# Rows' first turns, a split of two groups' sums, and the last tiles' sums made in PSUM, in a float32 pipeline of attention, MLP and role adapters

## The chip, the cores and the metric

The kernel runs on one NeuronCore of a Trainium2 chip. Its five engines are TensorE (PE, matmuls; PEld is its weight loads), VectorE (DVE), ScalarE (ACT), GpSimd (POOL) and SyncE (SP, which issues most DMAs). They run their own instruction streams and meet only at semaphores. The metric is the device time of one launch in microseconds; lower is better.

## The reference

64 sequences of 32 rows and 256 features, all float32. First an attention block with an MLP after it, then three role adapters, one after another:

```python
attn_out = softmax((x@Wq)(x@Wk)^T * V**-0.5) @ (x@Wv) @ Wp + bp
cms_out  = gelu(attn_out @ cW1 + cb1) @ cW2 + cb2 + one_hot(target_codes)
modifier = gelu(concat[attn_out, cms_out] @ mW1 + mb1) @ mW2 + mb2
x = clip(x + cms_out + modifier, 0, 1)
for layer in range(3):                      # weights chosen by each sequence's role (3 roles)
    u = gelu(x @ W_down[role] + b_down[role]) @ W_up[role] + b_up[role]
    x = layernorm(x + u) * gamma[role] + beta[role]
```

V is 256, the MLP's hidden width is 1024, the adapters' is 128.

## The kernel before

**Order of the rows.** A short routing stage counts the sequences of each role and finds a place for every sequence, so that nearly all blocks of 128 rows (a "window", 16 of them) hold one role. POOL then gathers the rows of `x` in that order (`gather`, eight indirect DMAs of 128 rows for the first two groups, semaphore `half_in[n]` for each pair).

**Start on PE.** `turn_weights(0..2)` transposes Wq, Wk, Wv. `fold_weights(0)` makes Wq Wk^T, `fold_weights(1)` makes Wv Wp. `half_part("X", n)` transposes 256 gathered rows into a bank, ACT copies them to `xT`, and `half_part("Y", n)` multiplies them with the folded matrix. `keep_busy` is a matmul of the identity whose result nobody reads.

**Main part.** The MLP works feature-major (features on partitions, rows along the free axis) on five groups of rows, `GROUPS`: three of 512 rows and two of 256. Every product of two float32 matrices is made of three matmuls of high and low parts (`mm3`). For a group, PE walks a list written out by hand, `core`: `("H", n)` makes the hidden block n (0 to 7 of cW1, 8 to 15 of mW1), ACT makes its GELU and its high part, DVE its low part, and `("D", n)` multiplies it with cW2 or mW2. Hidden blocks 8 and up need both `attn_out` (first half of the sum, "Ha") and `cms_out` (second half, "Hb"). `("C", 0)` is ACT's and DVE's step in which `cms_out` leaves PSUM: two sums on DVE (`cms`), two copies on ACT (`cms_hi`), two differences on DVE (`cms_lo`). `("F", 0)` sums x + cms_out + modifier on DVE into `cms` (semaphore `mod_summed`), step E clips it into `xT` (semaphore `x1_ready`).

**Adapters.** While group g+1 is in the MLP, the four windows of group g go through the adapters in its gaps, at spots of the same list (`SPOT`, `HALF`): PE's `downs` and `ups`, ACT's GELU, DVE's norm and POOL's power -0.5. A window's first `down` waits for `x1_ready` (`x1_needed`). Windows 8 to 11 belong to the third group of 512 rows.

**The end.** The windows 13, 14 and 15 are the list `LAST`; each has an object `Last` (called `one`, `two_`, `three` in the code) with two PSUM banks, `sum_bank` and `turn_bank`. Their residual is summed by PE: `last_residual` multiplies the identity with `x` into `sum_bank` and `last_up` adds the adapter's output. For layer 0 that `x` comes from `last_first_sum` (PE transposes the clipped rows into `sum_bank`) and `last_sum` (DVE adds the up-bias, writes `tail.x`). Window 13 starts within the last group's MLP, the other two after it. Its weights, norm rows and up-bias take the places of slots 1 to 3 of the windows before, so SP loads them late (`first_of_last`, seven DMAs in a row, semaphore `loaded`, the up-bias last).

Of the kernel before, what the change touches and what calls it, by code (L numbers as in the profile page):

```python
# [8 lines left out]
ALU = mybir.AluOpType  # L9
# [3 lines left out]
P = 128  # L13
# [43 lines left out]
def build(nc, x, codes, roles, Wq, Wk, Wv, Wp, bp, cW1, cb1, cW2, cb2, mW1, mb1, mW2, mb2, adapters, out):  # L57
# [3 lines left out]
    with ExitStack() as ctx:  # L61
# [281 lines left out]
        core += [("D", HB - 2), ("Ha", HB), ("D", HB - 1), ("C", 0), ("Ha", HB + 1), ("Hb", HB), ("Hb", HB + 1)]  # L343
# [6 lines left out]
        for g in range(NM):  # L350
            for step in core:
# [4 lines left out]
                steps.append((g, step))  # L356
        ATTENTION = {0: {("H", 10): ("X", 2), ("H", 11): ("Y", 2), ("H", 13): ("S", 2), ("H", 14): ("P", 2),
# [86 lines left out]
        def x1_needed(w):  # L444
            return PRIMED + VB * next(n + 1 for n, (first, rows) in enumerate(GROUPS) if (w + 1) * P <= first + rows)
# [16 lines left out]
        def store_batches(engine, of_last, quarters):  # L462
# [4 lines left out]
            def go():  # L467
                engine.wait_ge(tail.x_ready, tail.base + LAYERS + 1)
# [232 lines left out]
        def _(act):  # L701
# [103 lines left out]
            def last_part(stage_name, tail, layer):  # L805
                if stage_name == "turn":
                    act.wait_ge(tail.turned, layer + 1)
                    act.activation(tail.xT[:, :, :], two(tail.turn_bank[:, 0:V]), ACT.Copy).then_inc(tail.xT_ready, 1)
# [8 lines left out]
            chunks(0, 1)  # L817
            folded_weights(1)
            act.wait_ge(bias_turned, 1)
            act.activation(bias[:, :], bank[3][:, 0:22], ACT.Copy).then_inc(bias_ready, 1)  # L820
            half_part("X", 0)
            chunks(1, 2)
            half_part("Y", 0)
            half_part("X", 1)
# [47 lines left out]
        def _(dve):  # L872
# [107 lines left out]
            def part(step, n, g):  # L980
# [24 lines left out]
                if step == "F":  # L1005
                    dve.wait_ge(h_used, PRIMED + 2 * HB * (g + 1))
                    dve.wait_ge(base_ready, VB * (g + 1))
                    for vb in range(VB):
                        dve.scalar_tensor_tensor(cms[:, vb, rows], result_banks(g, HB)[vb][:, rows], bias[:, MB2 + vb:MB2 + vb + 1],
                                                 xT[:, vb, cols], ALU.add, ALU.add).then_inc(mod_summed, 1)  # L1010
                if step == "E":
                    for vb in range(VB):
# [45 lines left out]
            def last_sum(tail):  # L1058
                dve.wait_ge(tail.loaded, 16 * tail.loads)
                dve.wait_ge(tail.turned, 1)  # L1060
                if tail.left:
                    dve.wait_ge(*tail.left)
                dve.tensor_tensor(tail.x[:, :], tail.sum_bank[:, 0:V], tail.up_bias[:, :], ALU.add).then_inc(tail.x_ready, 1)

            def last_stats(tail, layer):
# [10 lines left out]
            def last_norm(tail, layer):  # L1076
                dve.wait_ge(tail.norm_step, 3 * (tail.base + layer) + 3)
                dve.wait_ge(tail.rstd_ready, tail.base + layer + 1)
# [496 lines left out]
```

## Time and profile before

| what | us |
|---|---|
| runs timed (3) | 365.42, 366.13, 367.71, median 366.13 |
| profiled execution, whole | 363.89 |
| span of its instructions | 362.1 |
| PE busy | 348.7 (96%) |
| DVE / ACT / POOL busy | 197.0 / 166.4 / 62.0 |

The span goes from the first instruction to the last; the profiled execution took 1.8 us more than it. All rows are of this one execution, 2.2 us shorter than the median. In the rows of the timeline the columns are: start in us from the start of the span, length in us, engine, line, operation, output<-inputs, shape, how many, and in brackets the engine's idle time just before and what ended it. The end of a matmul is modelled: a matmul of 256 columns is listed as 0.28 us though the next one starts 0.12 us later, so lengths of neighbours overlap by about 0.16 us and a real pause of PE is that much longer than the bracket says.

### The profile page before, as it was taken

To read this page: it belongs to the slowest core of one execution; us is meant where nothing else is said; L and a number is where in the kernel's file an instruction comes from. 1 tells how busy PE (TensorE), PEld (TensorE's weight loads), DVE (VectorE), ACT (ScalarE), POOL (GpSimd) and SP (SyncE) were. 2 spreads that over 40 slices of the span, in tenths; PEclk is the share of its full clock that TensorE was granted. 3 is DMA by queue.
4 is the path that set the end of the run, shared out by engine and by line. 5 is a ranking of instruction groups with operands and counts; after the bars stand their busy time and mean duration, and the time that the engine had idled before them with its cause. 6 is when DMAs were issued, how large, how long until landed. Compare 5 with 4: busy or idle time off the path is not lost.

```text
span 362.1 us, 6606 instructions
## 1 busy us (share of the span) xinstructions
PE 348.7 (96%) x2232; PEld 282.9 (78%) x2232; DVE 197.0 (54%) x477; ACT 166.4 (46%) x333; POOL 62.0 (17%) x94
## 2 busy tenths in 40 slices
PE   7889999999999999999999999999999999999994
PEld 6677688677876867888786777877899999989962
DVE  5057365420332746763535766554579777553584
ACT  3465685432652555452326454443455554533421
POOL 2700230000040101001311111003322025100231
PEclk9999999999999999999999999999999999999999
DMA  6663799175020223220076797602856543298001
GB/s 209 202 229 119 200 106 162 11 213 130 2 58 0 60 80 97 69 79 0 29 242 159 208 264 241 172 29 80 207 151 191 160 107 98 66 295 310 16 2 44
DMA packets 30646, 46.14 MB, mean 127 GB/s; under 512 B 4779, under 2 KB 15348, under 8 KB 30612
## 3 DMA queue, kind: packets, MB, share of 16 engines
q1 hardware_dynamic: 28852, 41.72, 42.6%
q0 software_dynamic: 1392, 3.80, 3.6%
q8 instruction: 18, 0.29, 0.4%
q10 hardware_dynamic: 368, 0.20, 0.2%
q14 instruction: 16, 0.13, 0.1%
HBM read 43.60 MB, written 4.48 MB: 133 GB/s over the span
## 4 chain that ended last, share of the span: by engine, by line
PE 85%; ACT 5%; DVE 4%; issue 3%; POOL 2%; DMA 1%; POOLq 0%; DVEq 0%; ACTq 0%
PE bank L312 11%; PE bank L314 10%; PE bank L313 10%; PE bank L1353 8%; PE bank L1358 8%; PE bank L1354 7%; PE bank L1277 4%; PE bank L1397 4%; PE bank L1376 3%; PE bank L1228 2%; PE bank L1267 2%; PE bank L1248 2%; ACT h_full L760 2%; PE bank L1428 2%; ACT h_hi L764 1%
## 5 line engine op out<-in xcount | busy, mean ns | idle before, releaser
L760 ACT ACTIVATE h_full<-bank,bias 128x512 f32<-128x512 f32 (+1 forms) x80 | 48.2, 602 | 114.4 <-PE bank L314 109.6
L985 DVE TENSOR_TENSOR h_lo<-h_full,h_hi 128x512 fp32r<-128x512 f32 (+1 forms) x80 | 46.7, 584 | 65.1 <-ACT h_hi L764 63.6
L683 POOL TENSOR_TENSOR rstd<-moments,minus_half 128x1 f32<-128x1 f32 x39 | 24.3, 624 | 174.2 <-DVE moments L1039 174.2
L764 ACT ACTIVATE h_hi<-h_full 128x512 fp32r<-128x512 f32 (+1 forms) x80 | 43.7, 546 | 2.6
L1031 DVE TENSOR_TENSOR window_y<-bank,window_x 128x256 f32<-128x256 f32 x39 | 16.5, 423 | 42.6 <-PE bank L1376 34.8
L1353 PE MATMUL bank<-h_hi,m_hi 128*128 128x512 f32 (+1 forms) x80 | 31.1, 397 | 0.4 <-ACT h_hi L764 0.3
L1353 PE MATMUL bank<-h_hi,c_hi 128*128 128x512 f32 (+1 forms) x80 | 30.8, 395 | 0.1
L312 PE MATMUL bank<-at_hi,m_hi 128*128 128x512 f32 (+1 forms) x80 | 29.5, 369 | 0.0
L312 PE MATMUL bank<-at_hi,c_hi 128*128 128x512 f32 (+1 forms) x80 | 29.4, 367 | 0.0
L314 PE MATMUL bank<-at_lo,c_hi 128*128 128x512 f32 (+1 forms) x80 | 27.8, 348 | 0.0
L314 PE MATMUL bank<-at_lo,m_hi 128*128 128x512 f32 (+1 forms) x80 | 27.8, 347 | 0.0
L313 PE MATMUL bank<-at_hi,c_lo 128*128 128x512 f32 (+1 forms) x80 | 27.7, 347 | 0.0
L313 PE MATMUL bank<-at_hi,m_lo 128*128 128x512 f32 (+1 forms) x80 | 27.7, 346 | 0.0
L1354 PE MATMUL bank<-h_hi,c_lo 128*128 128x512 f32 (+1 forms) x80 | 27.2, 348 | 0.0
L1354 PE MATMUL bank<-h_hi,m_lo 128*128 128x512 f32 (+1 forms) x80 | 27.1, 348 | 0.0
L655 POOL DMA_INDIRECT xr<-in_x,row_idx x16 | 16.4, 1022 | 62.7 <-PE bank L1267 52.9
L312 PE MATMUL bank<-cms_hi,m_hi 128*128 128x512 f32 (+1 forms) x70 | 24.5, 350 | 0.0
L314 PE MATMUL bank<-cms_lo,m_hi 128*128 128x512 f32 (+1 forms) x70 | 24.5, 350 | 0.0
L313 PE MATMUL bank<-cms_hi,m_lo 128*128 128x512 f32 (+1 forms) x70 | 24.3, 347 | 0.0
L1358 PE MATMUL bank<-h_lo,c_hi 128*128 128x512 f32 (+1 forms) x80 | 21.7, 352 | 0.2
L1022 DVE SCALAR_TENSOR_TENSOR window_x<-window_y,rstd,adapter_rows 128x256 f32<-128x256 f32 x39 | 18.8, 481 | 5.4 <-POOL rstd L683 3.7
L1358 PE MATMUL bank<-h_lo,m_hi 128*128 128x512 f32 (+1 forms) x80 | 21.4, 349 | 0.0
(216 smaller groups left out, 717.9 us busy)
## 6 DMA issues: line engine op xcount, KB each, us to landing
adapter_w<-packed_w SPq DMA_DIRECT2D x48, 256.5 KB, 3.5
adapter_rows<-packed_rows SPq DMA_DIRECT2D x36, 256.0 KB, 3.7
mixed_w<-packed_w SPq DMA_DIRECT2D x12, 256.5 KB, 4.6
stage<-in_L_cond_mW SPq DMA_DIRECT2D x6, 512.0 KB, 4.7
stage<-in_L_cond_cW SPq DMA_DIRECT2D x4, 512.0 KB, 6.5
last_w<-packed_w SPq DMA_DIRECT2D x2, 769.5 KB, 5.8
up_bias<-in_L_cond_b_up SPq DMA_DIRECT2D x12, 128.0 KB, 5.5
adapter_rows<-packed_rows SPq DMA_DIRECT2D x24, 64.0 KB, 3.2
```

Source lines behind the costliest of these rows:

```text
L312: pe.matmul(o, w_hi_ap, r_hi_ap, start=first, stop=False)
L313: pe.matmul(o, w_lo_ap, r_hi_ap, start=False, stop=False)
L314: return pe.matmul(o, w_hi_ap, r_lo_ap, start=False, stop=last)
L683: pool.tensor_tensor(slot.rstd[:, :], slot.moments[:, 1:2], minus_half[:, :], ALU.pow)\
L760: act.activation(h_full[:, n % 2, rows], bank[n % 2][:, rows], ACT.Gelu, bias=bias[:, b:b + 1])\
L764: act.activation(h_hi[:, n % 2, rows], h_full[:, n % 2, rows], ACT.Copy).then_inc(h_hi_ready, 1)
L985: dve.tensor_tensor(h_lo[:, n % 2, rows], h_full[:, n % 2, rows], h_hi[:, n % 2, rows].bitcast(F32), ALU.subtract).then_inc(h_lo_ready, 1)
L1022: dve.scalar_tensor_tensor(slot.x[:, :], slot.y[:, :], slot.rstd[:, :], slot.rows[:, 1, :], ALU.mult, ALU.add).then_inc(slot.x_ready, 1)
L1031: dve.tensor_tensor(slot.y[:, :], bank[6][:, 0:V], slot.x[:, :], ALU.add).then_inc(emptied[6], 1)
L1353: pe.matmul(results[ob][:, rows], high(cols), h_hi[:, n % 2, rows], start=(j == 0), stop=False)
L1354: pe.matmul(results[ob][:, rows], low(cols), h_hi[:, n % 2, rows], start=False, stop=False)
L1358: ins = pe.matmul(results[ob][:, rows], high(cols), h_lo[:, n % 2, rows], start=False, stop=(j == HB - 1))
```

## The change

1. Start, PE: `half_part("X", 0)` goes ahead of `fold_weights(1)`, `half_part("X", 1)` ahead of `half_part("Y", 0)`; one `keep_busy` of 64 columns goes. ACT's list is moved in the same way.
2. Main list: block 8's first half ("Ha") moves from between D6 and D7 to behind D7 and C, in all five groups.
3. Sums and clips (F, E) of the third group and of the last one are made in two parts of half the rows each, clip right behind sum, and `x1_needed` counts parts.
4. The last windows: a matmul of the identity with the up-bias opens `sum_bank` (`last_bias`), a true matmul with the identity adds the turned rows (`last_first_sum`), DVE's `last_sum` and layer 0's `last_residual` go. Window 13's block moves from behind D8 of the last group to behind Hb9.

```diff
-        core += [("D", HB - 2), ("Ha", HB), ("D", HB - 1), ("C", 0), ("Ha", HB + 1), ("Hb", HB), ("Hb", HB + 1)]
+        core += [("D", HB - 2), ("D", HB - 1), ("C", 0), ("Ha", HB), ("Ha", HB + 1), ("Hb", HB), ("Hb", HB + 1)]
...
+        def sum_parts(g):
+
+            return 2 if g == NM - 1 or g + 1 in CARRIED and GROUPS[g][1] == GR else 1
...
-                if step == "E":
-                    for vb in range(VB):
-                        dve.wait_ge(mod_summed, VB * g + vb + 1)
-                        dve.tensor_scalar(xT[:, vb, cols], cms[:, vb, rows], 0.0, 1.0, ALU.max, ALU.min)\
-                            .then_inc(x1_ready, 1)
+                if step in ("F", "E"):
+                    share = size // sum_parts(g)
+                    for part_n in range(sum_parts(g)):
+                        rows = slice(part_n * share, (part_n + 1) * share)
+                        cols = slice(first + part_n * share, first + (part_n + 1) * share)
+                        if step == "F":
+                            for vb in range(VB):
+                                dve.scalar_tensor_tensor(cms[:, vb, rows], result_banks(g, HB)[vb][:, rows],
                                                         bias[:, MB2 + vb:MB2 + vb + 1], xT[:, vb, cols], ALU.add, ALU.add)\
                                    .then_inc(mod_summed, 1)
+                        if step == "E" or sum_parts(g) > 1:
+                            for vb in range(VB):
+                                dve.wait_ge(mod_summed, summed(g) + VB * part_n + vb + 1)
+                                dve.tensor_scalar(xT[:, vb, cols], cms[:, vb, rows], 0.0, 1.0, ALU.max, ALU.min)\
+                                    .then_inc(x1_ready, 1)
...
-            def last_sum(tail):
-                dve.wait_ge(tail.loaded, 16 * tail.loads)
...
-            keep_busy(1, P // 2)
...
+            def last_bias(n):
+                tail = last[n]
+                pe.wait_ge(tail.loaded, 16 * tail.loads)
+                pe.matmul(tail.sum_bank[:, 0:V], ident[:, :], tail.up_bias[:, :], start=True, stop=False)
+
             def last_first_sum(n):
                 tail, w = last[n], LAST[n]
                 for vb in range(VB):
-                    ins = pe.transpose(tail.sum_bank[:, vb * P:(vb + 1) * P], xT[:, vb, columns(w)], ident[:, :])
-                ins.then_inc(tail.turned, 1)
+                    pe.matmul(tail.sum_bank[:, vb * P:(vb + 1) * P], xT[:, vb, columns(w)], ident[:, :],
+                              start=False, stop=False)
...
-                if g == NM - 1 and step == ("D", HB):
+                if g == NM - 1 and step == ("Hb", HB + 1):
                     pe.wait_ge(cms_copied, VB * NM)
-                    pe.wait_ge(last[0].loaded, 16 * last[0].loads)
+                    last_bias(0)
                     pe.wait_ge(x1_ready, x1_needed(LAST[0]))
+                    last_first_sum(0)
                     last_down(0, 0)
-                    last_first_sum(0)
                 if g == NM - 1 and step == ("D", HB + 2):
-                    last_residual(0, 0)
                     last_up(0, 0)
```

PE at the start, from the last product of the routing stage on (`raw,wT` is fold_weights(1), `ident,xr` the rows' turns X, `xT,fold` the products Y). Before:

```order
L1206 MATMUL bank6<-onehot,own_id 1x12
L1169 MATMUL bank2<-raw,wT 128x256 x4
L1471 MATMUL bank3<-ident,bias_rows 128x22
L1219 MATMUL bank4<-ident,xr0 128x128 x4
L1228 MATMUL bank0<-xT,fold 128x256 x4
L1219 MATMUL bank5<-ident,xr0 128x128 x4
L1228 MATMUL bank1<-xT,fold 128x256 x4
```

and now:

```order
L1215 MATMUL bank6<-onehot,own_id 1x12
L1228 MATMUL bank4<-ident,xr0 128x128 x4
L1178 MATMUL bank2<-raw,wT 128x256 x4
L1486 MATMUL bank3<-ident,bias_rows 128x22
L1228 MATMUL bank5<-ident,xr0 128x128 x4
L1237 MATMUL bank0<-xT,fold 128x256 x4
L1237 MATMUL bank1<-xT,fold 128x256 x4
```

The first turn of rows stands ahead of the fold and of the biases' turn, and the two products Y follow each other.

PE in the last group, from the last matmul of hidden block 9 to the first of block 10 (the six of bank2 and bank3 are D8; bank4 and bank5 are window 13's banks). Before:

```order
L314 MATMUL bank1<-cms_lo,m_hi 128x256
L1353 MATMUL bank2<-h_hi,m_hi 128x256
L1354 MATMUL bank2<-h_hi,m_lo 128x256
L1353 MATMUL bank3<-h_hi,m_hi 128x256
L1354 MATMUL bank3<-h_hi,m_lo 128x256
L1358 MATMUL bank2<-h_lo,m_hi 128x256
L1358 MATMUL bank3<-h_lo,m_hi 128x256
L1455 MATMUL bank5<-xT,adapter_w2 128x128 x2
L1434 MATMUL bank4<-ident,xT 128x128 x2
L312 MATMUL bank0<-at_hi,m_hi 128x256
```

and now:

```order
L314 MATMUL bank1<-cms_lo,m_hi 128x256
L1443 MATMUL bank4<-up_bias1,ident 128x256
L1448 MATMUL bank4<-ident,xT 128x128 x2
L1469 MATMUL bank5<-xT,adapter_w2 128x128 x2
L1362 MATMUL bank2<-h_hi,m_hi 128x256
L1363 MATMUL bank2<-h_hi,m_lo 128x256
L1362 MATMUL bank3<-h_hi,m_hi 128x256
L1363 MATMUL bank3<-h_hi,m_lo 128x256
L1367 MATMUL bank2<-h_lo,m_hi 128x256
L1367 MATMUL bank3<-h_lo,m_hi 128x256
L312 MATMUL bank0<-at_hi,m_hi 128x256
```

Window 13's block stands ahead of D8, with a bias product (up_bias1) that waits for `loaded`; its layer 0 residual product (window_x1 with ident, two steps later) is gone.

PE behind the last MLP step (bank4 and bank5 are window 13's, bank0 and bank6 window 14's, bank1 and bank7 window 15's). Before:

```order
L1455 MATMUL bank5<-window_y2,adapter_w2 128x128 x2
L1463 MATMUL bank4<-adapter_w2,window_y3 128x256
L1455 MATMUL bank6<-xT,last_w1 128x128 x2
L1434 MATMUL bank0<-ident,xT 128x128 x2
L1455 MATMUL bank7<-xT,last_w2 128x128 x2
L1434 MATMUL bank1<-ident,xT 128x128 x2
L1448 MATMUL bank0<-last_x1,ident 128x256
L1463 MATMUL bank0<-last_w1,last_h1 128x256
L1448 MATMUL bank1<-last_x2,ident 128x256
L1463 MATMUL bank1<-last_w2,last_h2 128x256
```

and now:

```order
L1469 MATMUL bank5<-window_y2,adapter_w2 128x128 x2
L1443 MATMUL bank0<-last_up_bias1,ident 128x256
L1477 MATMUL bank4<-adapter_w2,window_y3 128x256
L1443 MATMUL bank1<-last_up_bias2,ident 128x256
L1469 MATMUL bank6<-xT,last_w1 128x128 x2
L1448 MATMUL bank0<-ident,xT 128x128 x2
L1469 MATMUL bank7<-xT,last_w2 128x128 x2
L1448 MATMUL bank1<-ident,xT 128x128 x2
L1477 MATMUL bank0<-last_w1,last_h1 128x256
L1477 MATMUL bank1<-last_w2,last_h2 128x256
```

The residual products of last_x1 and last_x2 became bias products, and these stand on both sides of window 13's up product, ahead of the two windows' first product.

## Rows read from the trace of the kernel before

**Rows 1.** The page: busy time of the engines; granted clock in 40 slices.

```profile
PE 348.7 (96%) x2232; PEld 282.9 (78%) x2232; DVE 197.0 (54%) x477; ACT 166.4 (46%) x333; POOL 62.0 (17%) x94
...
PEclk9999999999999999999999999999999999999999
```

**Rows 2.** Timeline of the start, PE and DVE.

```profile
7.03 0.25 DVE L917 TENSOR_SCALAR onehot<-batch_id,rs 64x64 f32<-64x64 f32 x1
...
7.71 0.31 PE L1194 MATMUL bank<-onehot,own_id 64*32 64x16 f32 x8
...
7.95 3.35 PE L1169 MATMUL bank<-wT 128*128 128x256 f32 x8
...
11.86 1.99 PE L1169 MATMUL bank<-raw,wT 128*128 128x256 f32 x8
...
13.79 0.24 PE L1471 MATMUL bank<-ident,bias_rows 22*128 22x22 f32 x1
...
14.51 0.66 PE L1219 MATMUL bank<-ident,xr 128*128 128x128 f32 x4 [0.49 <-DMA xr<-in_x,row_idx]
...
15.86 1.99 PE L1228 MATMUL bank<-xT,fold 128*128 128x256 f32 x8 [0.69 <-ACT xT L723]
...
19.02 1.99 PE L1228 MATMUL bank<-xT,fold 128*128 128x256 f32 x8 [0.74 <-ACT xT L723]
...
21.70 0.50 PE L1260 MATMUL bank<-xT,yz 128*32 128x32 f32 x34 [0.25 <-ACT yz L727]
```

**Rows 3.** Timeline of the first group's middle, PE and DVE.

```profile
64.03 0.62 PE L1358 MATMUL bank<-h_lo,c_hi 128*128 128x512 f32 x2
...
64.76 1.29 DVE L993 TENSOR_TENSOR cms<-bank,cms_bias 128x512 f32<-128x512 f32 x2 [3.22 <-PE bank L1358]
...
66.26 0.47 PE L1312 MATMUL bank<-cms_hi,m_hi 128*128 128x512 f32 x1 [0.22 <-ACT cms_hi L768]
...
67.83 0.39 PE L312 MATMUL bank<-cms_hi,m_hi 128*128 128x512 f32 x1
```

**Rows 4.** Timeline where the third group ends, DVE and PE.

```profile
262.81 1.40 DVE L1009 SCALAR_TENSOR_TENSOR cms<-bank,bias,xT 128x512 f32<-128x512 f32 x2
...
264.13 0.84 DVE L1014 TENSOR_SCALAR xT<-cms 128x512 f32<-128x512 f32 x2
...
264.88 0.98 DVE L985 TENSOR_TENSOR h_lo<-h_full,h_hi 128x256 fp32r<-128x256 f32 x2
...
265.06 0.68 PE L1397 MATMUL bank<-xT,adapter_w 128*128 128x128 f32 x4 [0.61 <-issue]
...
266.06 0.40 PE L1358 MATMUL bank<-h_lo,c_hi 128*128 128x256 f32 x2
```

**Rows 5.** Timeline of the last group's middle, SP's queue and PE.

```profile
318.92 0.33 SPq L550 DMA_DIRECT2D up_bias<-in_L_cond_b_up  x1
...
323.39 0.39 PE L1353 MATMUL bank<-h_hi,m_hi 128*128 128x256 f32 x1 [0.30 <-ACT h_hi L764]
...
324.51 0.68 PE L1455 MATMUL bank<-xT,adapter_w 128*128 128x128 f32 x4
...
325.17 0.36 PE L312 MATMUL bank<-at_hi,m_hi 128*128 128x256 f32 x1
```

**Rows 6.** The tile up_bias from 315 to 328 us: that one DMA, issue to landing.

```profile
DMA to landing us min/median/max: 5.5/5.5/5.5
```

**Rows 7.** Timeline behind the last MLP step, PE and DVE.

```profile
342.49 0.70 PE L1463 MATMUL bank<-adapter_w,window_y 128*128 128x256 f32 x2 [0.46 <-ACT window_y L811]
...
343.02 0.64 PE L1455 MATMUL bank<-xT,last_w 128*128 128x128 f32 x4
...
345.01 0.59 PE L1463 MATMUL bank<-last_w,last_h 128*128 128x256 f32 x2
...
345.68 0.42 DVE L1067 BATCH_NORM_STATS2 last_stats<-bank 128x6 f32<-128x256 f32 x1
```

**Rows 8.** The chain that ended last, 341.5 to 346.2 us: start, length, what.

```profile
345.17 0.43 PE bank L1463 x2
```

More of the change, by code:

```diff
@@ L356, in build, with summed @@
                 steps.append((g, step))
+        def sum_parts(g):
+            return 2 if g == NM - 1 or g + 1 in CARRIED and GROUPS[g][1] == GR else 1
+        def summed(g):
+            return VB * sum(sum_parts(n) for n in range(g))
         ATTENTION = {0: {("H", 10): ("X", 2), ("H", 11): ("Y", 2), ("H", 13): ("S", 2), ("H", 14): ("P", 2),
@@ L444, in x1_needed @@
         def x1_needed(w):
-            return PRIMED + VB * next(n + 1 for n, (first, rows) in enumerate(GROUPS) if (w + 1) * P <= first + rows)
+            n, (first, rows) = next((n, group) for n, group in enumerate(GROUPS) if (w + 1) * P <= sum(group))
+            part = ((w + 1) * P - first - 1) * sum_parts(n) // rows
+            return PRIMED + summed(n) + VB * (part + 1)
         def result_banks(g, n):
@@ L806, in last_part @@
                 if stage_name == "turn":
-                    act.wait_ge(tail.turned, layer + 1)
+                    act.wait_ge(tail.turned, layer)
                     act.activation(tail.xT[:, :, :], two(tail.turn_bank[:, 0:V]), ACT.Copy).then_inc(tail.xT_ready, 1)
@@ L817, in _ @@
             chunks(0, 1)
+            half_part("X", 0)
             folded_weights(1)
@@ L1056, in eps_sets, with last_stats @@
                     dve.memset(tile.stats[:, 8:9], V * EPS).then_inc(eps_ready, 1)
-            def last_sum(tail):
+            def last_stats(tail, layer):
                 dve.wait_ge(tail.loaded, 16 * tail.loads)
[L1060 to L1065, printed above, removed]
                 dve.wait_ge(tail.up_done, layer + 1)
@@ L1078, in last_norm @@
                 dve.wait_ge(tail.rstd_ready, tail.base + layer + 1)
+                if layer == 0 and tail.left:
+                    dve.wait_ge(*tail.left)
                 dve.scalar_tensor_tensor(tail.x[:, :], tail.y[:, :], tail.rstd[:, :], tail.rows[layer][:, 1, :],
@@ L1099, in _ @@
                     part("E", 0, g - 1)
-                if g + 1 in CARRIED and step == ("F", 0):
+                if g + 1 in CARRIED and step == ("F", 0) and sum_parts(g) == 1:
                     part("E", 0, g)
@@ L1121, in _ @@
                     dve.wait_ge(eps_ready, 2 * SLOTS)
-                if g == NM - 1 and step == ("H", HB + 2):
-                    last_sum(last[0])
                 if g == NM - 1 and step == ("H", HB + 4):
@@ L1173, in _, with keep_busy @@
             pe.wait_ge(ident_ready, 1)
-            def keep_busy(n, columns=P):
+            def keep_busy(n):
                 for _ in range(n):
-                    pe.matmul(bank[6][:, 0:columns], ident[:, :], ident[:, 0:columns], start=True, stop=True)
+                    pe.matmul(bank[6][:, 0:P], ident[:, :], ident[:, :], start=True, stop=True)
             keep_busy(2)
@@ L1446, in last_residual @@
                 tail = last[n]
-                pe.wait_ge(tail.x_ready, tail.base + layer + 1)
+                pe.wait_ge(tail.x_ready, tail.base + layer)
                 pe.matmul(tail.sum_bank[:, 0:V], ident[:, :], tail.x[:, :], start=True, stop=False)
@@ L1523, in _ @@
             for n in (two_, three):
-                pe.wait_ge(last[n].loaded, 16 * last[n].loads)
+                pe.wait_ge(x1_ready, x1_needed(LAST[n]))
                 last_down(n, 0)
                 last_first_sum(n)
-            for n in (two_, three):
-                last_residual(n, 0)
-                last_up(n, 0)
+            last_up(two_, 0)
+            last_up(three, 0)
             last_turn(one, 2)
```

32 lines of the change are left out of this document (14 added, 18 removed).

## Prediction

> **What bounds the kernel now.** I read the page first: PE is busy 96% of the span at a granted clock of full speed in every slice [rows 1]. So the time is PE's work plus its pauses, and an edit is worth only what it takes from a pause or from PE's own list. DVE, ACT and POOL have room on average; they matter where PE waits for them. Then I went through the timeline at each place that the diff touches and looked at PE's bracket (what it waited for), adding 0.16 us for each bracket because the listed ends overlap. Last I read the chain behind the last MLP step. All numbers are against the profiled execution, 363.89 us (span 362.1 and 1.8 around it); the median of the runs, 366.13, lies 2.2 higher, and I add the same difference to the median.
>
> **1. The start: about +0.05 us.** In the profile the first turn of rows starts at 14.51, when the gather has landed, and the scores (L1260) start at 21.70: 7.19 us. In it PE pauses twice for ACT's copy of xT, 0.69 and 0.74 in the brackets, 0.85 and 0.90 in truth. The fold of Wv (1.99 listed) and the biases' turn run from 11.86 to 14.0, before the gather lands, so they cost nothing today [rows 2]. The new order puts them behind the first turn. That fills both pauses, but the fill is longer than they are: 7.19 - 0.85 - 0.90 + 1.93 (from 11.86 to 13.79) + 0.1 = 7.47, or +0.25 with the two pauses gone entirely. ACT gets its copies in time: the second one has a whole product Y before it. On the other side, without `keep_busy` the place product (L1194 at 7.71) can follow the one-hot of 7.03 + 0.25 = 7.28, about 0.35 earlier [rows 2], and the gathers go out that much earlier. Whether the last of them lands earlier is not shown, since the weights' DMAs share the engines: between 0 and 0.35, and I take 0.2. Sum +0.05, bounds -0.1 and +0.25. ACT's and DVE's moved steps lie under PE's work.
>
> **2. The first half of block 8 behind D7: -0.55 us, in the first group alone.** There PE has D7 done at 64.03 + 2 x 0.23 = 64.49, then only block 9's six matmuls and block 8's second six; block 9's second half starts at 67.83. That is 3.34 for twelve matmuls of 0.23, 2.78: a pause of 0.56, because DVE's sums start at 64.76 and PE has its first cms_hi at 66.26 [rows 3]. With D7 1.39 earlier DVE, which was idle 3.22 before this, starts at 63.4 and all of it is ready in time. D7 itself now follows D6 directly; its h_hi was ready long before in this group, since twelve small products stood in between. In the second, third and fourth groups the windows' products already stand between block 9 and block 8's second half, and PE has no pause at L1312 worth a row (the largest in the first group is the bracket of 0.22, in rows 3); in the last group DVE is in a window's norm until the sums start, so they would not start earlier, and item 4 swallows it. Bounds: 0 and -0.6.
>
> **3. The third group in two parts: -0.35 us.** Windows 8 and 9 wait for all of E: PE could have started at 264.29 and did at 265.06, a pause of 0.77 [rows 4]. DVE needs 1.40 listed for two sums of 512 and 0.84 for two clips. By halves I take 0.40 for a sum of 256 and 0.20 for a clip, so a part takes 1.2 to 1.3: windows 8 and 9 are free at 264.1, and the pause goes. But DVE ends the second part at about 265.3 in place of 264.9, and the low part of the next hidden block stands behind it (0.42 of its row). It is ready at 265.7; PE, now earlier, wants it 1.0 after the window's product (265.06 to 266.06) [rows 4], at 265.3. So 0.44 comes back as a new wait at the h_lo matmul of D1: -0.77 + 0.44 = -0.33. Bounds -0.77 and 0.
>
> **4. Window 13's block ahead of D8: +0.85 us.** This is the one edit that meets a DMA. The block must wait for `loaded`, and its last DMA, the up-bias, is issued at 318.92 and takes 5.5: 324.4 [rows 5, 6]. Today the block starts at 324.51, so it just waits for that DMA, after D8. D8 itself paused 0.46 (bracket 0.30) at 323.39 for h_hi; PE was free at 322.93. In the new order PE stands at the bias product from 322.9 on, and D8 is queued behind it. SP's issues hang on window 12's first norm, long before, so they don't come earlier. From 324.51: bias product 0.43 (the chain's time for two pieces of that size [rows 8]), turned rows as four pieces 0.45 and the down product 0.45 (its four pieces are listed with 0.68, less the overlap), D8 0.71: block 10 starts at 326.5 in place of 325.17, +1.3. The residual product of layer 0 two steps later is gone, -0.43. Sum +0.87. From here to the last MLP step PE has no pause that could take it back. Bounds: -0.8 (the DMAs are in early: the pauses of 0.46 and 0.35 go, the true matmuls cost 0.23) and +1.3.
>
> The turned rows were transposes and are now true products. The rows have 0.66 for the down product and both transposes [rows 5], so 0.21 for these, against 0.45: +0.24 for each of three windows, counted here and below. The Trainium skill (TensorE: Matmul & The Clock Gate, Terms) says that the transpose mode is four times faster for float32; by that the new ones would take 0.8, and the total would be 1.2 us higher. I go by the row of the down product, which has the same shape, and no run here shows the ratio yet.
>
> **5. The end: +0.15 us.** Today window 14's product starts at 343.02, right after the clips; its up product starts at 345.01 and DVE's statistics, from which DVE's own list bounds the rest, at 345.68. In the new list window 14's bias product hides in PE's wait for ACT (0.46 before 342.49), but window 15's stands behind the up product: 342.49 + 0.43 + 0.43 = 343.35, later than 343.02 [rows 7, 8]. The clips by tiles come before today's 343.02, too early to be of use. Then four products of 0.45 (down, turned rows, twice) lead to window 14's up product at 345.17: +0.16. Window 15's comes 0.35 earlier, but DVE is still at window 14. DVE loses its two sums of 0.42, which stood in waits. Bounds -0.4 (if the sums were on the chain) and +0.6.
>
> **Sum.** 0.05 - 0.55 - 0.35 + 0.87 + 0.16 = +0.18 us: 364.1 against 363.89, and 366.3 against the median of 366.13. No change that can be measured: within 1% (3.7 us), which is about what a measurement of this kernel tells from none.
>
> **Rivals.**
> A. The loads of window 13 are no bound (they land as PE arrives, or what PE waited for at 324.51 was something else). Then item 4 is -0.8 and the sum -1.5: 364.6. For it: the bracket there names no DMA. Against: landing and start agree within 0.1 us, and the block's own data were ready long before. Chance 0.2.
> B. PE's clock falls at the start: slower. Now PE has work until 14.0, then a pause of half a us. In the new list nothing stands between the routing products (they end at 11.86 today, so about 11.5) and the rows' landing (14.2 to 14.5), a pause of 2.7 to 3.0 us. Eight matmuls of one shape took 3.35 from 7.95 and 1.99 from 11.86 [rows 2], so the first ran mostly at 1.2 GHz and the second at 2.4, though the page shows full clock in every slice. If this pause sends the clock back, the fold and the first Ys run at the low level: +1.36 for each such block, two of them 2.7, total +2.9, 369.0. It decides from the point at which PE's next block is listed with over 3 us. For: the clock had to be earned at the start. Against: the pause is the only one, and PE's pause behind item 4 is shorter. Chance 0.13. The Trainium skill (TensorE: Matmul & The Clock Gate, the section on HAM oscillation) warns that a wait for DMA between bursts, if it is long enough, makes the next burst start at the low level; by that rule B is what happens if this pause is long enough, and no row of this profile holds a pause in mid-kernel to try it on.
> C. The change doesn't do what it says: the gathers land no earlier, the split only moves the wait, the tail's products cost more. Then 0.25 - 0.55 + 0 + 1.0 + 0.6 = +1.3: 367.4. Chance 0.12.
> The forecast has 0.5, and 0.05 is left for what I don't see.
>
> **Range and chances.** A to C span 364.6 to 369.0. The upper end of B is left out; the medians of the few runs differ by some 0.7 to either side (365.42 to 367.71). Range 364.0 to 368.3. Faster by over 1% needs -3.7 us, more than all lower bounds together (-2.7): 0.05. Slower by over 1% needs B and C at once: 0.06. Within 1%: 0.89.
>
> **What the new profile would show.** The fold of Wv listed with 1.99 between two turns of rows, and the scores near 21.8 (3.3 for the fold: B). No bracket before L1321 in the first group. No pause before the first adapter product behind the third group, but one before the h_lo matmul of D1. A pause of 1.5 to 2 us before L1443 in the last group, ended by the up-bias's landing; without it, A. Window 15's bias product just ahead of L1469. I am wrong if the loads come earlier with the rest of PE's list, or if a pause of PE that I called filled shows up elsewhere.

## The result, and the profile after

| | before | after |
|---|---|---|
| median of 7 executions each, us | 365.42 (363.49 to 367.71) | 368.94 (366.74 to 370.20) |
| profiled execution (span), us | 363.89 (362.1) | 370.20 (368.4) |

The ratio is 1.0088 [1.0053, 1.0124]: slower by 0.9%, outside the range of 364.0 to 368.3. In all tables below the medians hold every execution; the ratios leave out those over 1.5% above the fastest of their kernel. Every execution also reports the mean clock granted to TensorE, 1.0 standing for 2.4 GHz. That of the seven of after was .983 to .990, and of the profiled one .984. The profiled execution of before had 1.0. The mean leaves out the start: before has it at 1.0 although the eight matmuls from 7.95 on are listed with 3.35 for the 1.99 of the next eight [rows 2].

The page of after, busy time and granted clock in 40 slices (the lines of before are [rows 1]):

```profile
PE 351.9 (96%) x2236; PEld 286.4 (78%) x2236; DVE 196.6 (53%) x482; ACT 166.7 (45%) x333; POOL 62.0 (17%) x94
...
PEclk9999997899999999999999999999999999989999
```

PE is as busy as before by share and 3.2 us longer in time with four matmuls more. The clock row shows why: slices 7, 8 and 36 are below full. Windows of after show the two places (columns: from:to, length, PE busy with its count, PEclk, DMA share, GB/s):

```profile
50.00:57.00 7.00, 7.00 (x31) 1.00 1.11 121
60.00:67.00 7.00, 7.00 (x21) 0.53 0.49 83
67.00:74.00 7.00, 6.92 (x30) 1.00 0.40 118
320.00:326.00 6.00, 6.00 (x46) 1.00 0.95 270
329.50:332.80 3.30, 3.30 (x17) 0.50 0.76 273
333.00:339.00 6.00, 6.00 (x51) 1.00 0.70 287
```

The busy column can't show it: PE is listed as busy throughout, or nearly (6.92 of 7.00 at the least), in every row, with fewer matmuls where the clock is 0.5 (1.2 GHz). Now the timeline of PE in after, place by place. The start (before: [rows 2]):

```profile
13.98 0.66 PE L1228 MATMUL bank<-ident,xr 128*128 128x128 f32 x4 [3.22 <-DMA xr<-in_x,row_idx]
14.48 1.89 PE L1178 MATMUL bank<-raw,wT 128*128 128x256 f32 x8
...
16.96 1.89 PE L1237 MATMUL bank<-xT,fold 128*128 128x256 f32 x8
19.07 1.99 PE L1237 MATMUL bank<-xT,fold 128*128 128x256 f32 x8 [0.22 <-issue]
...
21.75 0.76 PE L1269 MATMUL bank<-xT,yz 128*32 128x32 f32 x64 [0.25 <-ACT yz L738]
```

The scores start at 21.75 against 21.70: +0.05, as forecast, and the fold at full rate. The match hides two misses that cancel: the rows landed 0.53 earlier (13.98 against 14.51, forecast 0.2), and from there to the scores it took 7.77 in place of 7.19, +0.58 where +0.25 was forecast. The first group's middle (before: [rows 3]):

```profile
57.69 3.18 PE L1298 MATMUL bank<-acol,prep_w 128*128 128x1 f32 x24
60.73 0.77 PE L1362 MATMUL bank<-h_hi,c_hi 128*128 128x512 f32 x1
...
64.29 0.63 PE L1362 MATMUL bank<-h_hi,c_hi 128*128 128x512 f32 x1
...
69.06 0.39 PE L1321 MATMUL bank<-cms_hi,m_hi 128*128 128x512 f32 x1
...
70.44 0.39 PE L312 MATMUL bank<-cms_hi,m_hi 128*128 128x512 f32 x1
```

L1298 is `down_biases`, 24 products with one moving column each, which the change doesn't touch. Within it the clock falls, and the 512-column matmuls behind it are listed with 0.63 for 0.39 until 66.6. This costs 3.2 us. The pause before L1321 is gone: block 9's second half starts at 70.44 against 67.83 in [rows 3], +2.6, where the matmuls ahead of the pause were at +3.2. The windows' gap and the third group's end (before: [rows 4]):

```profile
219.80 0.30 PE L1403 MATMUL bank<-adapter_w,window_xT 128*32 128x128 f32 x2 [1.20 <-DMA mixed_w<-packed_w]
...
268.14 0.60 PE L1406 MATMUL bank<-xT,adapter_w 128*128 128x128 f32 x4
...
269.50 0.50 PE L1367 MATMUL bank<-h_lo,c_hi 128*128 128x256 f32 x2 [0.28 <-DVE h_lo L996]
```

A load of a mixed window's weights is waited for (+1.3; none in the profiled execution of before). At L1406 0.81 is gained, and 0.45 given back at the h_lo matmul. The last group's middle (before: [rows 5]):

```profile
322.17 0.43 SPq L561 DMA_DIRECT2D up_bias<-in_L_cond_b_up  x1
...
328.14 0.67 PE L1443 MATMUL bank<-up_bias,ident 128*128 128x256 f32 x2 [1.96 <-DMA up_bias<-in_L_cond_b_up]
328.65 0.61 PE L1448 MATMUL bank<-ident,xT 128*128 128x128 f32 x4
329.09 0.71 PE L1469 MATMUL bank<-xT,adapter_w 128*128 128x128 f32 x4
329.46 0.56 PE L1362 MATMUL bank<-h_hi,m_hi 128*128 128x256 f32 x1
...
330.88 0.41 PE L312 MATMUL bank<-at_hi,m_hi 128*128 128x256 f32 x1
```

The up-bias lands 5.8 us after its issue, PE stands before it for 2.1, and 1.3 us after PE resumes the clock is at half for 3.4 us. Block 10 starts at 330.88 against 325.17, +5.7. The chain of the end in after (start, length, what):

```profile
346.33 0.22 PE bank L1456 x2
...
348.15 0.43 PE bank L1443 x2
...
350.18 0.45 PE bank L1448 x4
```

L1456 is a pair of transposes, L1448 the true products that took the place of such pairs. This settles the price of the change's products: 0.45 for 0.22, a factor of two. The Trainium skill (TensorE: Matmul & The Clock Gate, Terms) says that the transpose mode is four times faster for float32; this trace doesn't agree.

**Where the 6.3 us of the two profiles went** (shift of the same matmul's start, after minus before): start +0.05; fall of the clock at 59.8 +3.2; block 8's half -0.6; mixed_w +1.3; third group -0.35; last group's C -0.45; wait and true products of window 13's block net of the residual +1.5; fall behind it +1.5 (half clock from 329.46 to 332.87); tail +0.2.

### The profile page after: what moved, and what is told of

Its sections match the earlier page's. It is cut to its first block, busy times and chain, and to the rows that moved or that the text cites. A ratio compares the mean times of both kernels' runs of the same rounds, so it can differ in the third digit from the quotient of the medians.

```text
span 368.4 us, 6624 instructions
## 1 busy us (share of the span) xinstructions
PE 351.9 (96%) x2236; PEld 286.4 (78%) x2236; DVE 196.6 (53%) x482; ACT 166.7 (45%) x333; POOL 62.0 (17%) x94
## 4 chain that ended last, share of the span: by engine, by line
PE 72%; SPq 7%; DMA 5%; issue 5%; DVE 5%; ACT 3%; POOL 3%; POOLq 0%; DVEq 0%; ACTq 0%
PE bank L312 9%; PE bank L314 9%; PE bank L313 9%; PE bank L1362 6%; PE bank L1367 6%; PE bank L1363 6%; PE bank L1286 4%; PE bank L1406 3%; DMA mixed_w<-packed_w 3%; SPq L553 2%; PE bank L1385 2%; SPq L557 2%; PE bank L1276 2%; PE bank L1237 2%; PE bank L1257 2%
## 5 line engine op out<-in xcount | busy, mean ns | idle before, releaser
L1362 PE MATMUL bank<-h_hi,c_hi 128*128 128x512 f32 (+1 forms) x80 | 32.2, 412 | 0.1
L1363 PE MATMUL bank<-h_hi,c_lo 128*128 128x512 f32 (+1 forms) x80 | 28.1, 360 | 0.0
L1367 PE MATMUL bank<-h_lo,c_hi 128*128 128x512 f32 (+1 forms) x80 | 22.6, 364 | 0.5 <-DVE h_lo L996 0.3
```

What stands on the lines that cost most here:

```text
L1362: pe.matmul(results[ob][:, rows], high(cols), h_hi[:, n % 2, rows], start=(j == 0), stop=False)
L1363: pe.matmul(results[ob][:, rows], low(cols), h_hi[:, n % 2, rows], start=False, stop=False)
L1367: ins = pe.matmul(results[ob][:, rows], high(cols), h_lo[:, n % 2, rows], start=False, stop=(j == HB - 1))
```

## The experiments

Two theories stood at the outset. **Theory 1:** the pauses that the change makes or lengthens cost themselves and bring PE's clock down. **Theory 2:** the falls come by chance in both kernels, and only a pause costs. Each run has 12 executions (best_loads 8). The runs of one set (the recorded expectations say "call") were timed together with 31 to 35 executions of before, and share them; set 1 is the result above. "Clock" is the mean over them of the mean granted clock; .0047 of it is one stretch of 3.4 us at half, 1.7 us of PE's work. Not all of it is work, though: in the profile of after_again the clock is also at half from 362.73 to the end of the span at 365.50, where PE has nothing left to do. That is .0038 of the mean and costs nothing, and before's profile has none of it. So a difference of under .004 between two kernels need not be time.

| set | kernel | median us | ratio to before | clock | before's clock |
|---|---|---|---|---|---|
| 2 | b_again | 364.81 | 0.9989 [0.9962, 1.0016] | .9954 | .9942 |
| 2 | late_block | 365.77 | 1.0002 [0.9968, 1.0037] | .9905 | |
| 2 | filled_pause | 366.28 | 1.0025 [0.9995, 1.0056] | .9895 | |
| 2 | before_early | 365.40 | 1.0024 [0.9998, 1.0049] | .9949 | |
| 3 | after_again | 365.50 | 1.0017 [0.9982, 1.0052] | .9896 | .9939 |
| 3 | start_alone | 366.54 | 1.0035 [0.9999, 1.0071] | .9902 | |
| 3 | old_start | 364.60 | 0.9998 [0.9961, 1.0034] | .9931 | |
| 3 | old_start_spread | 362.49 | 0.9941 [0.9913, 0.9970] | .9976 | |
| 4 | start_filled | 367.73 | 1.0034 [1.0001, 1.0067] | .9924 | .9943 |
| 4 | after_spread | 365.66 | 0.9984 [0.9950, 1.0018] | .9914 | |
| 4 | before_spread | 364.66 | 0.9987 [0.9959, 1.0015] | .9954 | |
| 4 | spread_again | 364.37 | 0.9950 [0.9918, 0.9981] | .9943 | |
| 5 | after_third | 366.87 | 1.0065 [1.0034, 1.0096] | .9867 | .9960 |
| 5 | loads_first | 364.05 | 0.9985 [0.9951, 1.0020] | .9901 | |
| 5 | best_third | 363.06 | 0.9942 [0.9906, 0.9978] | .9957 | |
| 5 | best_loads | 361.98 | 0.9903 [0.9865, 0.9941] | .9970 | |

**The kernels unchanged: b_again, after_again, after_third.**

> The kernel before, unchanged, to see how often its own clock falls. Theory 1 (the pause that the change puts into the last group makes the clock fall there, and the kernel before is free of that): granted clock of every execution at 0.995 or more except where the stretch of tiny products at 58 to 60 us makes it fall (0.98 to 0.99 there); no fall behind 300 us. Theory 2 (the clock falls by chance, in both kernels alike): its executions show the same mean clock as the changed kernel's, 0.983 to 0.990.

> The kernel after, nothing changed, beside the same runs of the kernel before as the three that follow. Theory 1 (each long pause that the change makes on PE, at the start and in the last group, sends the clock back for a stretch): 368.0 to 369.5, mean clocks of the executions mostly .983 to .990, a profile with half clock behind the wait for up_bias in the last group. Theory 2 (the clock falls come by chance in both kernels alike, the first profile of it had many): 366.5 to 367.5, the profile without a fall in the last group, mean clocks spread as in the kernel before (.99 to 1.0).

> The kernel after unchanged, once more, so that the others of this call have it beside them. The ratio was 1.0088 in the first call and 1.0017 in the third. Theory 1 says that it follows the falls of the clock: mean clocks of .984 with the first ratio, of .990 with the second, and the time should again go with the mean clock.

b_again shows before against itself: no difference. The profile of b_again itself held one stretch of 3.4 us at half clock from 15.1 on, so falls at the start are no property of after alone. What differs is how often: 28 of after's 31 executions had a mean clock of .990 or less, and 15 of before's 136. After's time goes with it: seven executions at .982 to .984 took 368.75 to 370.20, three at .993 to .998 took 362.51 to 364.04. It isn't the whole, since two executions of b_again with a clock of 1.0 took 363.55 and 366.16. So the ratio moves from set to set, 1.0088, 1.0017, 1.0065. Both later medians of after, 365.50 and 366.87, lie inside the forecast range of 364.0 to 368.3: that the first lay outside it depended on how often the clock fell in those seven executions. The rest of b_again's expectation didn't come: theory 1 had .995 or more but for falls near 60 us, where its twelve executions have .991 to 1.0 and its profile a fall at the start. Theory 1 was right on the clocks of after_again (nine of twelve at .990 or less) and missed its median by 2.5 us (365.50 where it had 368.0 to 369.5); theory 2's 366.5 was missed too, and the fall that theory 1 wanted in the last group is not in the profile. The PE rows of after_again:

```profile
14.39 0.99 PE L1228 MATMUL bank<-ident,xr 128*128 128x128 f32 x4 [4.06 <-DMA xr<-in_x,row_idx]
15.18 3.28 PE L1178 MATMUL bank<-raw,wT 128*128 128x256 f32 x8
...
326.72 0.67 PE L1443 MATMUL bank<-up_bias,ident 128*128 128x256 f32 x2 [1.65 <-DMA up_bias<-in_L_cond_b_up]
```

Here the fold is listed with 3.28 for 1.89, which is rival B as the prediction drew it, behind a wait of 4.06. Behind the wait of 1.65 no clock fell. after_third repeats both (4.12 and 3.10 at the start, 2.05 at L1443 with no fall).

**Window 13's block: late_block, filled_pause, before_early.**

```diff
 late_block (after):   if g == NM - 1 and step == ("D", HB):             # was ("Hb", HB + 1)
 before_early (before): if g == NM - 1 and step == ("Hb", HB + 1):        # was ("D", HB)
 filled_pause (after):  + 4 x pe.matmul(bank[5][:, 256:512], ident, cms[:, 0, 0:256])   # ahead of last_bias(0), unused
```

> The changed kernel, window 13's block (bias product, turned rows, down product) put back behind D8 of the last group, all else kept. Theory 1: the pause of 2.0 us ahead of L1443 shrinks to some 0.4, no clock fall at 320 to 335 us, 2.5 to 3.0 us faster than the changed kernel (median 366.0 to 366.4). Theory 2: only the pause goes, 1.2 us faster (367.7), and clocks stay at 0.983 to 0.990.

> The changed kernel with four products of the identity with 256 columns (0.43 us each, result not read) ahead of window 13's block, so that PE works through 1.7 us of its pause. Theory 1: same wait for the up-bias's landing in all, but no clock fall behind it, 1.7 us faster than the changed kernel (367.2). Theory 2: no change of time (368.9), since the block starts at the same landing.

> The kernel before with one edit: window 13's down product and transposes ahead of D8 in place of behind it. Theory 1: a pause of about 1.6 us before L1455, a clock fall behind it, 0.6 (pause less D8's own) plus 1.7 (clock) = 2.3 us slower than before. Theory 2: 0.6 us slower.

late_block's wait for the up-bias is 0.63, filled_pause's 0.55, and neither profile has a fall there. before_early, whose wait was 1.41, had none either: theory 1 missed there. Its ratio, +0.9 us with an interval from -0.1 to +1.8, leaves out theory 1's 2.3 us and agrees with theory 2's 0.6. late_block is level with before. After was not run in this set, so its gain over after is only by the ratios (1.0002 against 1.0088, 1.0017, 1.0065), as is filled_pause's (1.0025), and neither is clear of 1.0017. The medians, 365.77 and 366.28, are below what either theory had for them.

**The start: start_alone, old_start, start_filled.**

```diff
 start_alone (before) / old_start (late_block), PE and ACT:
  new:  X0, fold_weights(1), bias turn, X1, Y0, Y1
  old:  fold_weights(1), bias turn, X0, Y0, X1, Y1     (and keep_busy of 64 columns)
 start_filled (after): + 9 x pe.matmul(bank[2][:, 0:P], ident, ident)    # ahead of half_part("X", 0), behind the wait
                                                                         # for wT_copied, which moves up with them
```

> The kernel before with the new start alone (first turn of rows ahead of the fold of Wv, second ahead of the first product Y, keep_busy of 64 columns gone). Theory 1 (the pause of 3 us at the start sends the clock back): +0.05 for the order and +1.0 to +1.7 for one or two more stretches of 3.4 us at half clock between 13 and 20 us, so 366.1 to 366.8; the fold listed with over 3 us. Theory 2 (falls at the start come by chance): 365.0 to 365.3, as before.

> The kernel after with window 13's block behind D8 (as in late_block) and with the start of before (the fold of Wv and the biases' turn ahead of the first turn of rows, keep_busy back). What is left of the change: block 8's first half behind D7, the split groups, the tail's bias products. Theory 1 (the 3 us pause ahead of the first rows makes the clock fall there more often than the kernel before's 0.5 to 1.3 us): falls at 13 to 20 us as seldom as in before, 363.9 to 364.7 where before has 365.1, some 1.2 less than late_block. Theory 2 (the order at the start has no part in the falls): as late_block, 365.3 to 366.0, falls at the start in as many executions.

> The kernel after with nine products of the identity with itself (128 columns, nobody reads them, about 0.22 us each) between the routing products and the first turn of rows, in the 3 to 4 us in which PE waits there for the gather. Nothing else is changed and no real work comes earlier. Theory 1 (the clock falls at the start because PE stands still there): a listed wait under 1.5 us, no half clock between 13 and 20 us in the profile, mean clocks up by one or two stretches of 3.4 us (from .987 to .991 or more), 1.2 to 2.0 less than after (365.5 beside 364.4 for before), so about 0.3 us either side of before. Theory 2 (the fall at the start comes from the order, the DMAs or by chance, not from the standing still): mean clocks as in after, .987 to .989, no gain, up to 0.3 slower.

start_alone brings the clock from .9939 to .9902, nearly all of what after_again lost (.9896), and is 2.1 us slower by the medians, 1.3 by the ratio (whose interval just touches 1): theory 1's 366.1 to 366.8. Its first wait is 3.88 and its fold listed with 3.29. Its profile has half clock from 14.2 to 17.6 and again from 62.0 to 65.4, so the difference isn't the fall at the start alone. old_start takes the new start out of late_block. The clock rises as theory 1 has it, .9931 for .9905, but the time is 0.2 over the median of its set's before, where 0.4 to 1.2 under it was expected (0.9998 against late_block's 1.0002 in another set). start_filled is split too. Its profile, PE and ACT (it is of an execution of 370.68, where the fastest took 364.18, so it may not stand for the others):

```profile
11.64 0.69 PE L1209 MATMUL bank<-onehot,code_rep 64*128 64x64 f32 x2
...
12.53 2.27 PE L1482 MATMUL bank<-ident 128*128 128x128 f32 x18
14.64 0.60 PE L1228 MATMUL bank<-ident,xr 128*128 128x128 f32 x4
15.08 1.89 PE L1178 MATMUL bank<-raw,wT 128*128 128x256 f32 x8
...
17.10 0.60 ACT L734 ACTIVATE xT<-bank 128x512 f32<-128x512 f32 x1 [3.82 <-remote]
```

With the pause filled the fold runs at full rate and the clock rose to .9924, as theory 1 says; but the time did not follow: 1.0034, where 0.3 us to either side of before was expected. Two visible parts: the routing product of L1209, ahead of the filler, came at 11.64 (9.62 in after_again) because the eight matmuls of fold_weights(0) before it are listed with 3.78 for 2.00, ahead of anything that the edit adds; and ACT made its first copy at 17.10 though the turn was done at 15.24. Why ACT stood still for these 1.9 us the profile doesn't say.

**The tiny products: old_start_spread, after_spread, before_spread, and old_start_spread again as spread_again and best_third.**

```diff
-                if g == 0 and step == ("H", 7):
-                    down_biases()                 # 24 products of 128x1 in a row
+                if g == 0 and step in BIAS_AT:    # H7, D7, Ha8, Ha9, Hb8, Hb9
+                    down_bias(BIAS_AT[step])      # four products each; DVE takes the sums behind Hb9 in place of H7
```

> old_start with one more edit: the 24 products of 128x1 for the adapters' down biases, which stand in one row behind H7 of the first group (2.7 us), go in six packets of four behind H7, D7, the two first halves and the two second halves of blocks 8 and 9, and DVE takes their sums later. PE's work is the same. Theory 1, widened (the stretch of tiny products makes the clock fall at 58 to 66 us when a fall is due): 0.4 to 1.2 less than old_start, no half clock at 58 to 66 us. Theory 2 (the fall there has nothing to do with the tiny products): the same as old_start within 0.3, and falls at 58 to 66 us in as many profiles. If each of the packets costs a switch of its own, 0.1 to 0.5 more than old_start.

> The kernel after with the 24 tiny products (128x1) in six packets of four instead of one row of 2.7 us. Theory 1 (a row of tiny products counts for the clock as standing still does): no half clock between 58 and 68 us, mean clocks up by .005 to .009, 1.5 less than after. Theory 2 (the fall near 60 us only repeats on some interval behind the fall at the start): still a fall near 60 us, time as after. The pause at the start and the wait for up_bias stay, with what they cost.

> The kernel before with the spread alone. Theory 1: its executions lose the one stretch of 3.4 us that most of them have (mean clocks .991 to .995 go to .998), 1.0 to 1.5 us faster, 363.0 to 363.6 beside 364.4. Theory 2: within 0.3 of before. Either way it says what of old_start_spread's gain (-1.9) comes from the spread and what from the change's own parts: by the traces' pauses these give -0.7.

> old_start_spread once more, unchanged, in another call. If its gain is the kernel's and not that call's, 0.993 to 0.996 of before, mean clocks .996 to 1.0.

> old_start_spread unchanged, beside the others of this call: 0.993 to 0.996 of before.

The row of products in old_start, where the clock holds:

```profile
56.80 2.73 PE L1299 MATMUL bank<-acol,prep_w 128*128 128x1 f32 x24
```

A window of after_spread, with the columns of PE, PEld, DVE, ACT and POOL ahead of PEclk, against the row 60 to 67 of after (0.53):

```profile
57.00:66.00 9.00, 9.00 (x46) 7.62 (x46) 6.81 (x9) 5.59 (x9) 0.00 (x0) 1.00 1.07 153
```

Over all profiles: with the new start and the products in a row the clock fell between 59.8 and 63.5 in seven of eight (late_block is the exception), with the old start and the row in none of four, and with the products spread in none of six, with either start (the new one in after_spread alone). So in these profiles the fall goes with both, the row of tiny products and the new start. That either is its cause is not shown. The runs moved the start and split the row, and with each edit the row's place in time moved too (it starts between 56.8 and 60.3); no run moves the unsplit row and keeps the rest. That the spread removes the fall rests on after_spread alone, since the old start never showed it, and after_spread's fall at the start was long (12.6 to 19.4) like late_block's (13.3 to 20.1), the one that had no fall near 60 with the row in place. Theory 2 of after_spread, a mere repetition behind the fall at the start, is out by other profiles: after and start_filled have the fall near 60 and none at the start, b_again has one at the start, the row, and none near 60. But the two aren't independent: in all five profiles that hold both, the second begins 47.8 us after the first. In time the spread alone is worth little to before (0.9987, whose interval holds 1; theory 1's 1.0 to 1.5 us faster and clock of .998 didn't come) and perhaps more on top of old_start in the same set (0.9941 against 0.9998, whose intervals overlap a little). after_spread's 0.9984 lies below after's three ratios, but after was not timed beside it. The kernel with both gave 0.9950 and 0.9942 in two further sets, as forecast. What it gains isn't mainly clock: in spread_again the clocks are .9942 and .9943, where .996 to 1.0 was expected, and best_third's profile, like before's without half clock while PE works, has a span of 360.6 against 362.1. Items 2 and 3 of the change are in it.

**The cause of the wait itself: loads_first, best_loads.**

```diff
+                load_up_bias(tail.up_bias[:, :], which, P, tail.first_loaded)
+                load_w(tail.w[0], which, 0, tail.first_loaded)
                 load_rows(tail.rows[0]..., tail.loaded)
                 for layer in range(1, LAYERS): load_w(..., tail.loaded); load_rows(..., tail.loaded)
-                load_up_bias(tail.up_bias[:, :], which, P, tail.loaded)
```

last_bias(0) waits for first_loaded (2 DMAs), window 13's `down` of layer 1 for the rest. best_loads is old_start_spread with this and with the block back ahead of D8.

> The kernel after with one edit: of window 13's seven loads the up-bias and layer 0's weights go first and count on a semaphore of their own, and its bias product waits for these two alone; the other five are waited for two layers later. So the up-bias is issued some 3 us earlier (3.1 in the profile of after, from 322.17 to 319.09), with a landing 5.5 to 6 us later at about the time when PE arrives. Theory 1 (the pause in the last group, 1.7 to 2.6 in the profiles of after, costs itself and in some executions a fall of the clock of 1.7): no listed wait of over 0.5 at the bias product, no half clock behind it, and 1.9 less than after plus the falls: 1.8 to 3.3 less than after_third. Theory 2 (the pause is taken back by later waits): within 0.5 of after_third.

> All in one: the change, with the start of before, the tiny products in six packets, and window 13's up-bias and first weights loaded first, so that its block can stand ahead of D8 as the change has it. By the sums: best_third (block behind D8) still has 0.6 to 1.05 of wait for the up-bias and the pause of 0.46 ahead of D8; both go: 0.8 to 1.5 less than best_third, 0.990 to 0.992 of before. By the rival (the DMAs that now follow behind delay what comes later) the same as best_third within 0.3.

In loads_first SP's issue and the product's start:

```profile
316.53 0.33 SPq L562 DMA_DIRECT2D up_bias<-in_L_cond_b_up  x1
...
323.50 0.59 PE L1449 MATMUL bank<-up_bias,ident 128*128 128x256 f32 x2
```

and in after_third:

```profile
319.72 0.33 SPq L561 DMA_DIRECT2D up_bias<-in_L_cond_b_up  x1
...
325.80 0.67 PE L1443 MATMUL bank<-up_bias,ident 128*128 128x256 f32 x2 [2.05 <-DMA up_bias<-in_L_cond_b_up]
```

No bracket is left. Timed side by side, the median falls by 2.8 us (366.87 to 364.05), the clock rises from .9867 to .9901, and the intervals of the two ratios overlap nowhere. That is theory 1's 1.8 to 3.3. By the profiles the block gains 1.9 of it, about the whole wait, and the rest agrees with falls that stay away (after_third had three executions at .982 and .983, loads_first none below .986). Ahead of the block the two profiles are 0.4 apart, behind it 2.3 and at the end 2.4, so nothing is taken back. The up-bias went out 3.2 us earlier and also landed faster, 3.3 us after its issue against 5.8 in after. The profiles with their waits at L1443: 1.96, 2.09 and 2.57 had half clock behind them; 2.05, 1.65 and everything shorter had none. So at this place a wait of about 2 us sometimes brings the fall. best_loads, 0.9903, is the fastest: 1.1 less than best_third, where 0.8 to 1.5 was expected, though with eight executions its interval and best_third's overlap.

## Why the prediction was wrong, point by point

The step that failed is what the forecast did with PE's clock: it put the clock's falls at nothing in the sum, gave them 0.13 as rival B, at the start only, and cut the range off below B. In the first profile two falls cost 4.7 of the 6.3 us (3.2 near 60 us, 1.5 behind the up-bias), neither at the start; at the start, where B had its fall, all seven further profiles of that start (unfilled) have one. Next to it stand a wait for a mixed window's weights (1.3) and item 4's term, 0.6 too small.

- **Item 1, the start: +0.05.** The number was right in the first profile by luck: an earlier landing (0.53 for 0.2) paid for an order that cost more (0.58 for 0.25; the sum written out as 7.47 is 0.28). The pause was about right (2.7 to 3.0 forecast, 3.22 listed there, 2.03 to 4.12 in the others). What failed is **rival B's chance of 0.13**: all seven further profiles with the new start unfilled had half clock between 12 and 20 us; only the first had none. Of the seven, five had one stretch of 3.4 us (1.7 us of work) and two had two, where B had two (2.7, 2.9 in all). start_alone is 2.1 us slower by the medians, with a second fall near 60 in its profile. My argument against B, that before's pause is the only one and short, used one profile of before in which the clock never fell; four of nine profiles with the old start had a fall there, behind waits of 0.79 to 1.31. The five without one had 0.69 or less.
- **Item 2: -0.55.** Right: -0.6.
- **Item 3: -0.35.** Right, both parts: -0.81 and +0.45 against -0.77 and +0.44.
- **Item 4: +0.87.** The mechanism was right: the up-bias's landing ends PE's wait, behind which D8 queues. The term was mis-sized, +1.5: PE arrives earlier by what C gained there (0.45, forecast 0), and the DMA took 5.83 for 5.5. Rival A (no bound) was wrong in every profile with the change's order of loads. And **the sentence "PE's pause behind item 4 is shorter" failed**: I used it as a reason against B and never priced a fall behind that pause. It came in the first profile (1.5 us) and in two of the four others with the change's block and order of loads and nothing filled ahead of it.
- **Item 5: +0.16.** Right: +0.2.
- **Not in the forecast at all:** the fall at `down_biases` (+3.2 in the first profile, 1.7 where it is one stretch), 36 us behind the nearest edited place ahead of it, whose cause stays open; and the mixed windows' weights, +1.3 in the first profile. The same kernel had no such wait in its two later profiles; b_again had none, before_early 0.85, filled_pause 1.93. No profile ties it to the change.
- **The sum.** Without the clock's falls and mixed_w the first profile gives +0.3; forecast was +0.18. The terms come that close partly because item 4's +0.6 too much stands against C's -0.45 in the last group. The range was too narrow upward because B was cut off from it and was priced as one place, where it fell at three.

What stays open: what brings the clock down near 60 us and why only with the new start, why start_filled got slower, and what makes after's clock differ between sets (.9856, .9896, .9867).

## What to carry to other kernels

In a kernel with PE at 96% of the span and a clock of 1.0 in its one profile, a pause of 2 us can cost more than 2 us: look at the mean clock of all executions before and after, not at the one profile. Before moving a block ahead of other work, look up which of its DMAs lands last and move that issue first; reordering the loads took 2.8 us from the same kernel. Where a row of tiny products stands in the program, try it spread between large ones: it cost nothing here, and no profile with the spread had a fall at that place. And when a forecast number comes out right, look whether its parts did: the start's +0.05 was made of two errors.

## What the runs showed of the hardware that was not expected

- Matmuls with one moving column leave PE listed as busy (24 in 2.73 us at full clock, 3.18 in after), and the clock fell within them or up to 1.0 us behind them in seven profiles of twelve. That they bring the fall about is not shown. PE busy of 7.00 in 7.00 at a clock of 0.53 is the row to remember.
- The clock's fall is not tied to a fixed pause: half clock behind waits of 0.79, 0.88, 0.97 and 1.31 at the start (best_loads, spread_again, before_spread, b_again), none behind 3.22 in the first profile of after. With the old start the nine profiles divide cleanly: a fall in the four with 0.79 or more, none in the five with 0.69 or less. The Trainium skill (TensorE: Matmul & The Clock Gate, HAM oscillation) warns of waits for a DMA between bursts of matmuls; these rows agree with the mechanism, and show it for waits that I had held harmless.
- Two transposes of 128x128 in float32 take 0.22 us, two true products with the identity 0.45.
